# Sparse cross-attention and experts: the thresholds of a head reach their rows of the query slot by two transfers instead of TensorE and ScalarE

## The reference, cut to what matters

```python
zs = -jnp.sort(-x, axis=-1)
cssv = jnp.cumsum(zs, axis=-1) - 1.0
support = zs > cssv / rho
k = jnp.maximum(jnp.sum(support, axis=-1, keepdims=True), 1)
tau = jnp.take_along_axis(cssv, k - 1, axis=-1) / k.astype(x.dtype)
return jnp.clip(x - tau, 0.0)
...
attn = sparsemax(scores)
out = jnp.einsum('bhqk,bhkd->bhqd', attn, vh)
```

## Time and profile before

| what | value |
|---|---|
| median of three runs | 7428.7 us (7425.35 to 7432.42) |
| the profiled execution | 7425.23 us, span 7423.3 us |
| busy over the span | PE 76%, DVE 81%, ACT 79%, POOL 30% |
| granted clock of PE, mean | 0.733 |
| attention | about 540 to 6250 us, 256 heads |

### The profile page before, as it was taken

The page is one execution under the profiler, slowest core; times in us unless marked ns, Lnnn a source line. Parts: engine busy times, 40 slices in busy tenths (PEclk is TensorE's granted clock), DMA queues, the critical chain, the costliest instruction groups (busy, mean ns, idle before and its releaser), DMA issues. The chain is left out here.

```text
span 7423.3 us, 165050 instructions
## 1 busy us (share of the span) xinstructions
PE 5646.4 (76%) x20864; PEld 1924.1 (26%) x20864; DVE 5977.4 (81%) x49467; ACT 5842.5 (79%) x13220; POOL 2210.4 (30%) x10037
## 2 busy tenths in 40 slices
PE   8976777776777777767777777677777775999999
PEld 5541111111111111111111111111111111666666
DVE  5559989999998999999999999899999995444443
ACT  2328999999999999999999999899999996222222
POOL 2223333333333333333333333333333332000000
PEclk9986666666666666666666666666666666999999
DMA  6651111111111111111111111111111112111110
GB/s 203 225 194 30 30 30 31 32 30 30 33 31 31 30 31 30 30 29 30 30 32 30 32 30 33 27 31 32 31 32 31 33 33 62 49 37 48 51 37 23
DMA packets 315591, 344.02 MB, mean 46 GB/s; under 512 B 113912, under 2 KB 238464, under 8 KB 314240
## 3 DMA queue, kind: packets, MB, share of 16 engines
q1 hardware_dynamic: 311936, 324.40, 15.9%
q0 software_dynamic: 2304, 8.39, 0.3%
HBM read 212.38 MB, written 120.10 MB: 45 GB/s over the span
## 5 line engine op out<-in xcount | busy, mean ns | idle before, releaser
L856 DVE MAX8 a_cand<-a_scores 128x8 f32<-128x42 f32 (+1 forms) x38912 | 4359.1, 193 | 296.2 <-issue 222.9
L619 ACT ACTIVATE a_junk_act<-a_cand,a_ntau 128x304 f32<-128x304 f32 (+1 forms) x4096 | 2066.8, 522 | 112.3 <-POOL a_ntau L931 50.5
L589 PE MATMUL a_ring<-a_q,a_k 99*128 99x512 bf16 (+1 forms) x3328 | 1478.7, 560 | 800.7 <-ACT a_scores L654 594.2
L534 PE MATMUL a_out<-a_attn,a_v 128*16 128x512 f32 (+1 forms) x6656 | 1404.2, 767 | 575.2 <-ACT a_attn L658 575.2
L654 ACT COPY a_scores<-a_ring 128x1024 f32<-128x1024 f32 (+1 forms) x2048 | 1612.2, 830 | 176.8 <-PE a_ring L585 110.1
L658 ACT ACTIVATE a_attn<-a_ring 128x1024 f32<-128x1024 f32 (+1 forms) x1792 | 1653.4, 974 | 2.5 <-PE a_ring L589 2.0
L585 PE MATMUL a_ring<-a_k,a_q 96*128 96x512 bf16 (+1 forms) x4096 | 1393.6, 471 | 71.6 <-DVE a_ident L679 32.9
L619 ACT ACTIVATION_READ_ACCUMULATOR a_junk_act<-a_cand,a_ntau 128x1 f32 x4096 | 845.6, 206 | 0.0
L585 PEld LDWEIGHTS a_ring<-a_k,a_q 96*128 96x128 bf16 x4096 | 391.9, 118 | 1472.7 <-issue 696.5
L589 PEld LDWEIGHTS a_ring<-a_q,a_k 99*128 99x128 bf16 (+1 forms) x3328 | 290.1, 119 | 1669.7 <-ACT a_scores L654 978.9
L1192 ACT ACTIVATE e_hid<-e_hid_ps,e_b_in 128x512 f32<-128x512 f32 x256 | 173.1, 687 | 667.7 <-PE e_hid_ps L1139 667.4
(11 more groups left out here) (171 smaller groups left out, 5777.0 us busy)
## 6 DMA issues: line engine op xcount, KB each, us to landing
a_k<-k_parts SPq DMA_DIRECT2D x1536, 50.0 KB
k_parts<-p_ks SPq DMA_DIRECT2D x48, 800.5 KB, 7.5
o_parts<-a_o SPq DMA_DIRECT2D x1024, 32.0 KB, 1.6
e_o<-o_parts SPq DMA_DIRECT2D x64, 512.0 KB, 6.6
p_ctx<-in_ctx_t SPq DMA_DIRECT2D x16, 1601.0 KB, 8.5
v_heads<-p_v SPq DMA_DIRECT2D x16, 1536.0 KB
a_q<-q_parts SPq DMA_DIRECT2D x1536, 16.0 KB
a_v<-v_heads SPq DMA_DIRECT2D x256, 96.0 KB
```

The costliest lines, as they stand in the source:

```text
L534: mm = nc.tensor.matmul(out_ps[at:at + HEAD_DIM], v_st[0:rows, u, c], attn[0:rows, k, (c % 2) * BANK:(c % 2 + 1) * BANK], start=c < 4, sto ...
L589: mm = nc.tensor.matmul(at[0:rows, m * BANK:(m + 1) * BANK], k_st[0:SCORE_ROWS + TAU_ROWS, ut, c * P:c * P + rows], q_st[0:SCORE_ROWS + TA ...
L619: ins = nc.scalar.activation(into[:, t].rearrange("p (a b) -> p a b", b=CHUNKS), cand[:, u % SLOTS, t, 0:w], ACT.Relu, bias=ntau[:, u % 2, ...
L856: ins = V.max(cand[:, u % SLOTS, t, :, c], scores[:, u % SLOTS, t, lo:hi])
```

## The change

PE's turn and ACT's cast are gone, and with them the identity, its load and its cast to bf16. `split` is written to a small tensor in the device's memory outside the core, `tau_rows` (two slots of 512 queries x 3 parts), by one DMA, and read back by a second DMA whose source is walked the other way: for each of the three parts, 512 elements of 2 bytes that lie 6 bytes apart. The second goes straight into rows 96 to 98 of the query slot. Both are issued by SP, which waits for `split` ahead of the first, for its landing ahead of the second, and, with the second, also for the read of the head before. SP's program is written step by step like those of the other engines; a step stores head i-4, loads head i+2 and then turns the thresholds of head i-2.

```diff
+            def turn_tau(i, u):
+
+                sp.wait_ge(tau_split, i + 1)
+                sp.dma_start(tau_rows[u % 2].rearrange("(t p) r -> p t r", p=P), split[:]).then_inc(tau_out, 16)
+                sp.wait_ge(tau_out, 16 * (i + 1))
+                if not isinstance(i, int) or i > 0:
+                    sp.wait_ge(tau_in_q, 16 * i)
+                sp.dma_start(q_st[SCORE_ROWS:SCORE_ROWS + TAU_ROWS, u], tau_rows[u % 2].rearrange("q r -> r q"), allow_slow_non_contiguous=True).then_inc(tau_in_q, 16)
+
+            def step(i, u):
+                if has(i, LAG + 1):
+                    done = i - LAG - 1
+                    store(done, (u - LAG - 1) % U)
+                    if not isinstance(i, int) or done + U < N:
+
+                        sp.wait_ge(products, NT * (done + 1))
+                        load(done + U, (u - LAG - 1) % U)
+                if has(i, 2):
+                    turn_tau(i - 2, (u - 2) % U)
...
-            def turn_tau(i):
-
-                pe.wait_ge(tau_split, i + 1)
-                if not isinstance(i, int) or i >= 1:
-
-                    pe.wait_ge(tau_in_q, i)
-                for t in range(TILES):
-                    mm = nc.tensor.matmul(turn_ps[SCORE_ROWS:SCORE_ROWS + TAU_ROWS, t * P:(t + 1) * P], split[:, t], ident[:], start=True, stop=True)
-                mm.then_inc(tau_turned, 1)
...
                         if (kind, n) == ("t", 0):
 
-                            pe.wait_ge(tau_in_q, i - LAG + 1)
+                            pe.wait_ge(tau_in_q, 16 * (i - LAG + 1))
...
-                        if (kind, n) == turn_at and do_t:
-                            act.wait_ge(tau_turned, i - LAG + 1)
-                            nc.scalar.copy(q_st[SCORE_ROWS:SCORE_ROWS + TAU_ROWS, ut], turn_ps[SCORE_ROWS:SCORE_ROWS + TAU_ROWS]).then_inc(tau_in_q, 1)
...
-            dve.wait_ge(ident_loaded, 16)
-            nc.vector.tensor_copy(ident[:], ident_f[:]).then_inc(setup, 1)
...
-                    pool.wait_ge(tau_turned, i)
-                    pool.sem_inc(passed_pool, 1)
+                    if not isinstance(i, int) or i > 0:
+                        pool.wait_ge(tau_out, 16 * i)
+                        pool.sem_inc(passed_pool, 1)
```

More of the change, by code:

```diff
@@ L349, in _, with attend_program @@
                 batch(BATCH - 2 + u, u, BATCH // 2 - 1, last=u == 1)
-def attend_program(nc, q_parts, k_parts, v_heads, ident_in, o_parts):
+def attend_program(nc, q_parts, k_parts, v_heads, tau_rows, o_parts):
     N = BATCH * HEADS
@@ L425, in attend_program @@
         zeros = sb("zeros", [P, 1])
-        ident_f = sb("ident_f", [P, P])
-        ident = sb("ident", [P, P], BF16)
         ones = sb("ones", [P, 1], BF16)
@@ L458, in attend_program @@
         loaded = [sem(f"loaded{u}") for u in range(U)]
-        ident_loaded = sem("ident_loaded")
         setup = sem("setup")
@@ L477, in attend_program @@
         pool_chain = sem("pool_chain")
-        tau_turned = sem("tau_turned")
+        tau_out = sem("tau_out")
         tau_in_q = sem("tau_in_q")
@@ L482, in attend_program @@
         general = sem("general")
-        SETUP = 5 + TILES
+        SETUP = 4 + TILES
         LOADS = len(K_PARTS) + len(Q_PARTS) + 2
@@ L489, in _ @@
         def _(sp):
-            sp.dma_start(ident_f[:], ident_in).then_inc(ident_loaded, 16)
             def load(i, u):
@@ L502, in store @@
                     sp.dma_start(o_parts[s, bass.ds(i * HEAD_DIM, HEAD_DIM)], o_sb[32 * s:32 * s + HEAD_DIM, u % 2]).then_inc(out_stored[u % 2], 16)
+            def turn_tau(i, u):
[14 more added lines that the diff above has]
+                    turn_tau(i - 2, (u - 2) % U)
             for i in range(U):
                 load(i, i)
[L506 to L517, removed]
+            walk(sp, step)
             for slot_stored in out_stored:
@@ L562, in step @@
                 order = groups(do_s, do_t)
-                turn_at = ("s", 1) if do_s else ("t", 0)
                 if has(i, LAG + 1):
@@ L570, in step @@
                     for kind, n, place in own:
-                        if (kind, n) == turn_at and do_t:
-                            turn_tau(i - LAG)
                         if (kind, n) == ("t", 0):
-                            pe.wait_ge(tau_in_q, i - LAG + 1)
+                            pe.wait_ge(tau_in_q, 16 * (i - LAG + 1))
                         seq = before(i) + place
@@ L1307, in program @@
     project_program(nc, x, ctx_t, wq, bq, wk, bk, wv, bv, ident, q_parts, k_parts, v_heads)
-    attend_program(nc, q_parts, k_parts, v_heads, ident, o_parts)
+    tau_rows = nc.dram_tensor("tau_rows", (2, QUERIES, TAU_ROWS), BF16).ap()
+    attend_program(nc, q_parts, k_parts, v_heads, tau_rows, o_parts)
     experts_program(nc, x, g_xattn, g_ffn, wo, bo, o_parts, router_w, w_in, b_in, w_out, b_out, ident, out)
```

## The result

| | before | after |
|---|---|---|
| median | 7429.03 us (4 runs) | 12749.67 us (4 runs, 12746.04 to 12762.91) |
| ratio of the times | | 1.7165, 95% interval 1.7136 to 1.7195 |
| profiled span | 7423.3 us | 12746.5 us |

What follows compares the result with a forecast made beforehand. A ring of dependences closing once per head, nearly as long as ACT's load, was taken as the bound. 255 x 8.0 us added to D = 2040 us on 7425.2 gave 9465, rounded to 9460 us; range 8150 to 13000.

Steps and rivals of the forecast that it cites:

- the ring A + D: Loop of dependences from one t0 to the next, closing once per head; claimed to be the period, mean 22.1 us.
- A: From PE's t0 to the end of the next head's `split`; forecast unchanged, 18.7 us without DVE's search, mean 19.8.
- D: Way of `split` into the query slot, up to the next t0; forecast to go from 2.3 to 10.3 us.
- SP sees `split` and issues: First step of the new D, from the end of `split` to SP's issue of the write; forecast 0.2 us.
- The write: `split` to the small tensor, 512 pieces of 6 bytes; forecast 2.0 us, then 0.2 for SP to issue the read.
- The read: 1536 elements into the query slot: 1.7 us fixed plus 512 per engine at 12 ns, 6.1; forecast 7.8 us.
- SP's order, costed at nothing: The next head's stores and loads behind SP's two issues; claimed free, counting only with a read of over 20 us.
- Slow elements: Rival for the read: 2-byte elements go singly at 20 to 42 ns or more, 10560 to 13620 us; chance 0.26.
- Spread or packed: Rival for the read: 96 elements per engine, 8215 us, or every element free, 7810 us; chance 0.15.
- Not slower: Rival: ACT sets the pace, PE's wait is cover, and ACT gains its cast, about 7277 us; chance 0.02.
- it leaves the time alone: Rival: a mix of the last two rivals where gain and loss cancel, 7425 us; chance 0.01.
- The fixed cost: Fixed part of each DMA in D: 1.6 and 1.7 us taken; the skill's 2.0 would give 9645 us.

Runs made afterwards that it cites:

- e11: Changed kernel with the write as 128 pieces of 24 bytes and the read as three runs of 1024 bytes, turn left out: 7675.7 us, ratio 1.0337.
- e9: Kernel before the change with LAG = 4 instead of 3 and two buffers for `split`: 7427.7 us over ten runs, ratio 1.0005.
- e5: Changed kernel with the rows of `tau_rows` 512 bytes apart instead of 6: 11815.1 us, ratio 1.5903.
- e13: Changed kernel, row 0 read as 509 elements on one engine, the other two rows as runs of 1024 bytes, their turn left out: 10540.6 us, ratio 1.42.
- e15: e11 plus a third transfer that t0 awaits: 3 x 512 elements of 2 bytes into partitions 0, 4 and 8 of an unread tile: 9618.7 us.
- e3: Changed kernel with the read cut into three one-row transfers, each spread over 16 DMA engines: 12176.0 us, ratio 1.6397.
- e4: Changed kernel with SP waiting for the read to land before it issues the next stores and loads: 12834.8 us, ratio 1.7284.
- e6: e1 plus a third transfer that t0 awaits: the same 1536 elements of 2 bytes into 128 partitions of an unread tile: 9399.9 us.
- e14: e11 plus a third transfer that t0 awaits: 3 x 512 elements of 2 bytes into partitions 0, 1 and 2 of an unread tile: 12010.9 us.
- e10: Changed kernel with the read as 768 elements of 4 bytes instead of 1536 of 2, turn left out: 9686.9 us, ratio 1.3045.
- e7: Changed kernel with LAG = 4 instead of 3, giving the thresholds one more step to arrive: 8564.8 us, ratio 1.1528.
- e1: Changed kernel with the read as three contiguous runs of 1024 bytes instead of 1536 elements of 2 bytes, turn left out: 8966.2 us, ratio 1.2074.

## Why the prediction was right in sign and wrong in size

**What bounds the kernel: half right.** The prediction set the ring A + D and ACT's load side by side and concluded that a longer D is not covered. It isn't: e11 lengthens D by 1.22 us and the period by 0.98. But the period of before is not set by the ring alone, since e9 opens the ring and keeps the time; ACT in its order, busy for 95%, is the likely bound, and the ring stood some 0.2 us behind. What the other 5% of ACT is was not taken apart. "The thresholds never arrive early" was too strong: its evidence was the wait for the cast, which e9 has as well, and the turn waited for `split` at 144 of 256 heads only.

**A: right.** 18.7 us was forecast in a head without DVE's search; the median after is 18.74. The mean was 0.28 us shorter than before, about as in e11. That gives 0.28 x 255 = 71 us back.

**SP sees `split` and issues: right in kind.** 0.03 us for 0.2, and nothing of its queue in the way.

**The write: mis-sized, 2.2 us forecast with SP's issue of the read, 5.73 measured.** The fixed part and the price by engine were nearly right where pieces lie apart (1.85 in e5). The missing 3.5 us comes from packed pieces of 6 bytes. The earlier trace rows showed 64-byte stores only, and nothing showed pieces that small.

**The read: the step that failed.** The prediction put its variable part as "the number of elements on one DMA engine times the price of one". Spread and price were right or nearly so, three engines and 12 ns: e13 measured 12.1 ns on one engine, and e15 14.9 on each of three, which would give 1.7 + 7.6 = 9.3 us instead of 7.8. The 12 was chosen between rows of 8.4 and 16 ns for other sizes and destinations, so that it came so near is in part luck. But in the query slot the elements on different engines don't pass side by side. Rows 96 to 98 take 9.7 ns for each of 1536 elements from three engines, and still 8.0 from sixteen, so 15.0 us and not 6.1. e3 refutes the form, e4 and e5 exclude the traffic behind and the source, e6 excludes the element as such, and e14 against e15 leaves the place of the destination. What there takes one element at a time, and why half as many elements of 4 bytes take a fifth of the time (e10), stays open.

**The sum.** In D the write gives +3.53, the read with PE's wake +9.89 (17.79 - 7.9), SP's wake -0.17: +13.25 us. D of before was 2.48 and not 2.3, -0.18, and A gives -0.28: together 12.79, times 255 is 3261. The unrounded forecast of 9465 becomes 12726. The first head's D is in no period but lies ahead of the first t0, which comes at 622.8 us after and 601.5 before, 21 us more: 12747. Measured: 12749.67.

**SP's order, costed at nothing: right here.** The four stores behind the read take 10.9 us to issue in the median step, 1.9 before, and e4 shows that even 18 us of waiting on SP costs 0.33 per head. The text said that a read of over 20 us would start to count; the real one of 17.8 stayed below. It counts in e7, where the ring no longer covers it.

**The rivals.** *Slow elements* came nearest in time: 9.7 ns shared by three engines is 29 ns on each, inside its 20 to 42. Its reason, that each engine is slow, isn't what the runs show: alone an engine takes 12. *Spread or packed* fell: e3 is what a spread read costs, 1.64. *Not slower* and *it leaves the time alone* are out by the result, and e11 shows why they had no room: D is near its least of 3.8 there and the ratio 1.034. Their condition, that ACT sets the pace, is what e9 speaks for; the cover they relied on is only 0.2 us.

**Signs named beforehand.** Packets higher by some 2000 per head: 2066. t0 waiting over 6 us at every head: 23. The write at 2 us, the read at 8, busy shares at 70% and the period at 30 were wrong by the same two terms. Of the signs against it, the read landing "in over 12 (elements are dear)" came.

**The fixed cost.** The prediction weighed 1.6 and 1.7 us from the earlier trace rows against the 2.0 of the Trainium skill ("DMA: Bandwidth & Descriptors", "Anatomy of one DMA"). In e11 the way from the write's issue to the read's is 1.53 and from the read's to t0 2.14, with the wakes. The first stays below the Trainium skill's figure and the second is close to it; either way it is not where 13 us went.

## What to carry to other kernels

Where a loop of dependences closes once per period and is about as long as the busiest engine's work, each microsecond that is put into its thin part beyond a small slack (0.2 us here) is paid in full, so measure that part before and cost every handoff in it. A transfer in single small elements is to be costed by where they land, not only by how many each DMA engine has: three neighbouring rows as destination made 15 us of 1536 elements, 128 partitions 1.7. Nothing tried here that goes through memory beats TensorE's turn and ScalarE's cast, 2.5 us in all; the best, e11, needs 3.7, and that is without the turn.

## What the runs showed of the hardware

- 2-byte elements into three neighbouring partitions share one limit: 9.7 ns each on three engines, 8.0 on sixteen; into three partitions 4 apart 5.0 each in all (14.9 per engine); into 128 partitions on sixteen engines 1.1. One engine alone into one row takes 12.1.
- 4-byte elements into the same rows take 3.7 ns, so a piece of half the size costs 2.6 times as much. Why is open.
- 512 packed pieces of 6 bytes are written in 5.7 us, the same 512 bytes apart in 1.85, and 128 packed pieces of 24 bytes in 1.5. Pieces that share a stretch of memory seem to wait for each other; the size at which that ends was not looked for.
- The packets' records can end long before a transfer lands: 4.6 us on average in the changed kernel, 9.9 in e3. A quiet DMA row doesn't mean that the data is there.
- SP can be held while it issues: its four stores behind the changed kernel's read take 10.9 us (median over the heads), 6.4 in e15, 1.8 in e1 and in e13, 1.9 before. What fills up was not looked for.
